# Differential attention and ternary FFN on one core: a head's difference, turns and copies half a head later, two-part fp16 scores

## The reference, cut to what matters

```python
q, k, v = LN(x) @ Wq.T, LN(x) @ Wk.T, LN(x) @ Wv.T      # 32 x 16, 16 x 16, 8 x 32
q, k = rope(q) * 16 ** -0.5, rope(k)
probs = softmax(q @ k.T + causal)                       # 32 score heads
diff = probs[:, :, 0] - lambda_full * probs[:, :, 1]    # 16 heads
attn = rmsnorm(diff @ v) * subln_weight * (1 - LAMBDA_INIT)
x = x + attn @ Wo.T
h = gelu(LN(x) @ ternary(w1).T + b1)
x = x + h @ ternary(w2).T + b2
```

## Time and profile before

| | |
|---|---|
| median of 3 runs | 4374.92 us |
| profiled execution, its own time | 4370.7 us |
| its span, first to last instruction | 4368.9 us |
| PE / DVE / ACT / POOL busy | 83 / 77 / 67 / 34 % |
| mean granted TensorE clock | 0.900 of 2.4 GHz |
| one image in the loop | 525.9 us |

### The profile page before, as it was taken

The page is one execution under the profiler, slowest core; times in us unless marked ns, Lnnn a source line. Parts: engine busy times, 40 slices in busy tenths (PEclk is TensorE's granted clock), DMA queues, the critical chain, the costliest instruction groups (busy, mean ns, idle before and its releaser), DMA issues.

```text
span 4368.9 us, 81035 instructions
## 1 busy us (share of the span) xinstructions
PE 3625.1 (83%) x23454; PEld 2157.1 (49%) x23454; DVE 3369.0 (77%) x6188; ACT 2913.5 (67%) x6786; POOL 1495.9 (34%) x1563
## 2 busy tenths in 40 slices
PE   2688888888888888888888988888888888888886
PEld 1345554455445454554545545555545555554553
DVE  6778967888678886788767887678877788678881
ACT  1567766777567775677756766667666777567772
POOL 0243234332333334332343324433134432333323
PEclk7788999989899899998889988999989989899998
DMA  4212112211122112212122110222122111222110
GB/s 133 54 25 41 24 43 43 40 23 33 35 43 43 23 38 46 43 25 38 26 43 43 36 31 23 47 37 43 25 44 43 32 31 25 44 43 43 20 37 14
DMA packets 146768, 166.71 MB, mean 38 GB/s; under 512 B 16640, under 2 KB 117632, under 8 KB 145792
## 3 DMA queue, kind: packets, MB, share of 16 engines
q1 hardware_dynamic: 146304, 161.13, 18.3%
HBM read 105.95 MB, written 55.12 MB: 37 GB/s over the span
## 4 chain that ended last, share of the span: by engine, by line
PE 41%; DVE 25%; issue 19%; ACT 8%; DMA 3%; SPq 2%; POOL 1%; DVEq 1%; ACTq 1%; POOLq 0%
DVE NM L667 9%; PE M L822 7%; PE M L872 7%; PE SP_ L837 6%; PE F L894 6%; PE DP L849 5%; PE F L907 4%; DVE E L691 3%; ACT E L543 3%; DVE CC L688 2%; DMA KST<-scratch 2%; PE M L816 2%; DVE NM L675 2%; PE SP_ L838 1%; PE DX L849 1%
## 5 line engine op out<-in xcount | busy, mean ns | idle before, releaser
L543 ACT ACTIVATE E<-SP_,NM 128x256 f32<-128x256 f32 (+7 forms) x2048 | 1518.3, 743 | 674.7 <-DVE NM L667 461.8
L667 DVE TENSOR_REDUCE NM<-SP_ 128x1 f32<-128x896 f32 (+3 forms) x1024 | 1034.2, 1018 | 257.8 <-PE SP_ L838 254.0
L837 PE MATMUL SP_<-KST,QST 96*128 96x512 bf16 (+3 forms) x3072 | 866.2, 356 | 394.5 <-ACT E L543 329.5
L691 DVE SCALAR_TENSOR_TENSOR E<-E,CC 128x512 f32<-128x512 f32 (+7 forms) x1024 | 928.6, 907 | 36.2
L555 ACT ACTIVATE DT<-DP 128x512 f32<-128x512 f32 (+3 forms) x1024 | 527.7, 515 | 534.9 <-PE DP L849 501.5
L849 PE MATMUL DP<-ident,E 128*128 128x128 f32 x3328 | 617.5, 304 | 140.4 <-DVE E L691 136.7
L675 DVE TENSOR_REDUCE NM<-SP_ 128x2 f32<-128x1024 f32 (+3 forms) x512 | 420.2, 821 | 309.2 <-PE SP_ L838 306.5
L837 PEld LDWEIGHTS SP_<-KST,QST 96*128 96x128 bf16 x3072 | 278.9, 103 | 745.7 <-ACT E L543 515.0
L894 PE MATMUL F<-X2H,W1Q 128*128 128x256 f16 x2048 | 512.1, 287 | 71.0 <-ACT HP L598 67.0
L849 PEld LDWEIGHTS DP<-ident,E 128*128 128x128 f32 x3328 | 395.6, 154 | 313.9 <-issue 164.3
L822 PE MATMUL M<-WQKV,WT 128*128 128x512 f32 x1040 | 531.7, 608 | 8.8 <-DVE T L650 4.1
(11 more groups left out here) (87 smaller groups left out, 4794.6 us busy)
## 6 DMA issues: line engine op xcount, KB each, us to landing
QST<-scratch SPq DMA_DIRECT2D x390, 128.0 KB, 4.4
scratch<-SPL SPq DMA_DIRECT2D x65, 576.0 KB, 2.8
KST<-scratch SPq DMA_DIRECT2D x390, 64.0 KB, 4.8
X<-in_x SPq DMA_DIRECT2D x66, 256.0 KB, 3.3
out<-SQ SPq DMA_DIRECT2D x64, 256.0 KB, 2.0
KST<-in_w1T SPq DMA_DIRECT2D x1, 4096.0 KB, 19.4
DT<-in_w2T SPq DMA_DIRECT2D x1, 4096.0 KB, 28.8
WQKV<-in_wqT SPq DMA_DIRECT2D x1, 1024.0 KB, 6.9
```

Source lines behind the costliest of these rows:

```text
L543: act.activation(dst, score_out(i, 2 * n + k, w), ACT.Exp, bias=NM[:, (2 * u + k) % 8:(2 * u + k) % 8 + 1], scale=1.0, accum_out=SUM[:, i ...
L667: nc.vector.tensor_reduce(NM[:, m:m + 1], score_out(i, 2 * n + k, P * (i + 1)), AX.X, ALU.max, negate=True).then_inc(max_ready, 1)
L691: nc.vector.scalar_tensor_tensor(out=E1[:, u % 2, 0:w], in0=E2[:, e:e + w], scalar=CC[:, u % 2:u % 2 + 1], in1=E1[:, u % 2, 0:w], op0=ALU. ...
L837: pe.matmul(SP_[:, k[a // 512], 0:n], q, KST[0:ROWS, a // P:(a + n) // P, kk, :], start=True, stop=not last)
```

## The change

Scores: q and k are split into two fp16 parts, high and rest, with scaled copies (rest times 64, high by 64), three products of 16 dimensions. Two score heads that share a KST column stand below each other (48 rows each), and QST holds zeros in the rows of the other one, so a score matmul still has 96 rows and the same columns. POOL's split becomes two `tensor_scalar`, the second from fp16 to fp16. The bytes of `QST`'s and `KST`'s DMAs halve at the same count of DMAs.

Order: `diff(s-1)` moves from h = 0 to h = 1 of step s; `diff_transposes(s-1)` from h = 1 of step s to h = 0 of step s+1; the copies go to h = 0 and h = 1 of that step; `half_v` follows half a step later. `E1` gets four rows, `E2` two in every tile, `R2` and `CC` four places. `exp(s,0)` waits for the turn of s-4 and `exp(s,1)` for `diff(s-2)`. The coefficient is still computed on DVE by the same two instructions.

Side jobs move one half step later, with these exceptions: `LN1_STATS`, `LN1_ROWS`, the FFN's places and `LN2_REST` (31) stay, `LN1_TURN` moves by two. Setup: w1 is loaded by four DMAs, as KST is half as large, and POOL clears QST. The diff, cut to its core:

```diff
-PROD = 6
-QPART = (0, 0, 0, 1, 1, 2)
-KPART = (0, 1, 2, 0, 1, 0)
-ROWS = PROD * DH
+PROD = 3
+QPART = (0, 2, 1)
+KPART = (0, 1, 2)
+PART = PROD * DH
+ROWS = 2 * PART
+LOW = 64.0
...
-LN1_STATS, LN1_ROWS, LN1_TURN = 1, 3, 4
-Q_PROJ, Q_ROPE = (7, 8, 9, 10), 11
-KV_PROJ, KV_ROPE = (12, 13, 14, 14), 15
-Q_TURN, Q_REST, K_TURN, K_REST = 16, 17, 20, 21
-V0_MOVE = 5
-PV_OUT = (19, 3)
-SUM_INVERSE, AT_TURN, AT_ROWS = 5, 6, 6
-MEAN_SQ, RMS_ROWS, AN_TURN = 9, 13, 22
-O_PROJ, O_SUM = (23, 24, 25, 26), 27
-LN2_STATS, LN2_ROWS, LN2_TURN, LN2_REST = 27, 29, 30, 31
+LN1_STATS, LN1_ROWS, LN1_TURN = 1, 3, 6
+Q_PROJ, Q_ROPE = (8, 9, 10, 11), 12
+KV_PROJ, KV_ROPE = (13, 14, 15, 15), 16
+Q_TURN, Q_REST, K_TURN, K_REST = 17, 18, 21, 22
+V0_MOVE = 6
+PV_OUT = (20, 4)
+SUM_INVERSE, AT_TURN, AT_ROWS = 5, 7, 7
+MEAN_SQ, RMS_ROWS, AN_TURN = 10, 14, 23
+O_PROJ, O_SUM = (24, 25, 26, 27), 28
+LN2_STATS, LN2_ROWS, LN2_TURN, LN2_REST = 28, 30, 31, 31
...
-        KST = sb("KST", [P, TILES, NK, P], BF16)
-        QST = sb("QST", [P, 2, NQ, P], BF16)
+        KST = sb("KST", [P, TILES, NK // 2, P], F16)
+        QST = sb("QST", [P, 2, NQ, P], F16)
         V = sb("V", [P, TILES, DKV], F32)
-        E1 = sb("E1", [P, 2, S], F32)
-        E2 = sb("E2", [P, S], F32)
+        E1 = sb("E1", [P, 4, S], F32)
+        E2 = sb("E2", [P, 2, S], F32)
         DT = sb("DT", [P, TILES, HALF, P], F32)
         NM = sb("NM", [P, 8], F32)
         SUM = sb("SUM", [P, 2, 2, H], F32)
-        R2 = sb("R2", [P, 2], F32)
+        R2 = sb("R2", [P, 4], F32)
         RS = sb("RS", [P, H], F32)
-        CC = sb("CC", [P, 2], F32)
+        CC = sb("CC", [P, 4], F32)
...
-        SPL = sb("SPL", [P, 3, D + DKV], BF16)
+        SPL = sb("SPL", [P, 3, D + DKV], F16)
...
-            sp.dma_start(w1f.rearrange("p (k n) -> p k n", k=KD), w1T.rearrange("(k p) n -> p k n", p=P)).then_inc(w1_in, 16)
-            sp.dma_start(w2f.rearrange("p (k n) -> p k n", k=FT), w2T.rearrange("(k p) n -> p k n", p=P)).then_inc(w2_in, 16)
+            for k in range(KD):
+                sp.dma_start(w1f[k], w1T[P * k:P * (k + 1), :]).then_inc(w1_in, 16)
+            sp.dma_start(draw.rearrange("p (k n) -> p k n", k=FT), w2T.rearrange("(k p) n -> p k n", p=P)).then_inc(w2_in, 16)
...
-                hold(sp, stacked, 16 * 2 * PROD * (nb - 1))
+                hold(sp, stacked, 64 * PROD * (nb - 1))
                 hold(sp, split_done, 2 * nb + 2)
                 sp.dma_start(scratch[tile % 2], SPL[:, :, :]).then_inc(scr_out, 16)
                 hold(sp, scr_out, 16 * nb + 16)
                 src = scratch[tile % 2].rearrange("(s d) a (c n) -> a d s c n", d=DH, n=P)
                 hold(sp, s_ready, q_free)
-                for j in range(PROD):
-                    sp.dma_start(QST[DH * j:DH * (j + 1), tile % 2, :, :].rearrange("p (s c) n -> p s c n", s=8),
-                                 src[QPART[j], :, :, 0:4, :]).then_inc(stacked, 16)
+                for a in range(2):
+                    for j in range(PROD):
+                        r = PART * a + DH * j
+                        sp.dma_start(QST[r:r + DH, tile % 2, :, :].rearrange("p (s c) n -> p s c n", s=8)[:, :, 2 * a:2 * a + 2, :],
+                                     src[QPART[j], :, :, 2 * a:2 * a + 2, :]).then_inc(stacked, 16)
                 if k_free is not None:
                     hold(sp, s_ready, k_free)
-                for j in range(PROD):
-                    sp.dma_start(KST[DH * j:DH * (j + 1), tile, :, :].rearrange("p (s c) n -> p s c n", s=8),
-                                 src[KPART[j], :, :, 4:6, :]).then_inc(stacked, 16)
+                for a in range(2):
+                    for j in range(PROD):
+                        r = PART * a + DH * j
+                        sp.dma_start(KST[r:r + DH, tile, :, :], src[KPART[j], :, :, 4 + a, :]).then_inc(stacked, 16)
...
+            pool.memset(QST[:, :, :, :], 0.0).then_inc(q_zeros, 1)
...
-                pool.tensor_scalar(SPL[:, 1, c], T2[:, c], 1.0, 0.0, ALU.mult, ALU.add).then_inc(mid_part, 1)
-                after(pool, mid_part, 2 * nb + part + 1)
-                pool.tensor_tensor(SPL[:, 2, c], T2[:, c], SPL[:, 1, c], ALU.subtract).then_inc(split_done, 1)
+                pool.tensor_scalar(SPL[:, 1, c], T2[:, c], LOW, 0.0, ALU.mult, ALU.add)
+                pool.tensor_scalar(SPL[:, 2, c], SPL[:, 0, c], 1.0 / LOW, 0.0, ALU.mult, ALU.add).then_inc(split_done, 1)
...
-                    old = T.before(n - 2)
+                    old = T.before(n - 4)
                     if old:
                         pb, pi, pn = old
                         after(act, t_ready, pb * N_T + tg(pi, pn, groups(pi) - 1) + 1)
-                    dst = E1[:, u % 2, 0:w]
+                    dst = E1[:, u % 4, 0:w]
                 else:
 
-                    after(act, d_ready, b * N_U + u - (1 if i < 4 and u > 0 else 0))
-                    e = 512 * (u % 2) if i < 4 else 0
-                    dst = E2[:, e:e + w]
+                    after(act, d_ready, b * N_U + u - 1)
+                    dst = E2[:, u % 2, 0:w]
...
-                    old = T.before(s - 1) if h else T.before(s - 2)
+                    old = T.before(s - 2)
                     if T.attend:
                         exp(T, s, h)
-                    if old and (h == 1 or groups(old[1]) == 2):
-                        dt_copy(*old, 1 - h)
+                    if old and (h == 0 or groups(old[1]) == 2):
+                        dt_copy(*old, h)
...
-                nc.vector.scalar_tensor_tensor(out=E1[:, u % 2, 0:w], in0=E2[:, e:e + w], scalar=CC[:, u % 2:u % 2 + 1],
-                                               in1=E1[:, u % 2, 0:w], op0=ALU.mult, op1=ALU.add).then_inc(d_ready, 1)
+                nc.vector.scalar_tensor_tensor(out=E1[:, u % 4, 0:w], in0=E2[:, u % 2, 0:w], scalar=CC[:, u % 4:u % 4 + 1],
+                                               in1=E1[:, u % 4, 0:w], op0=ALU.mult, op1=ALU.add).then_inc(d_ready, 1)
...
-                    if h == 0 and T.before(s - 1):
+                    if h == 1 and T.before(s - 1):
...
-                kk = ((s // 2) % 8) * 2 + (s // 2) // 8
+                kk = (s // 2) % 8
...
-                done = T.before(s - 2)
+                done = T.before(s)
...
-                    if h == 1:
-                        if T.before(s - 1):
-                            for g in range(groups(T.before(s - 1)[1])):
-                                diff_transposes(*T.before(s - 1), g)
-                        half_v(T, s, 1)
+                    if h == 0:
+                        if T.before(s - 2):
+                            for g in range(groups(T.before(s - 2)[1])):
+                                diff_transposes(*T.before(s - 2), g)
+                        half_v(T, s - 3, 1)
...
                     if h == 0:
                         scores_ahead(T, s + 1)
-                        half_v(T, s, 0)
+                    else:
+                        half_v(T, s - 2, 0)
```

More of the change, by code:

```diff
@@ L331, in diff_attention_ffn @@
         wsum = E1[:, 1, 0:2 * 64].rearrange("p (a b) -> p a b", b=64)
-        w1f = KST[:, :, :, :].rearrange("p a b c -> p (a b c)").bitcast(F32)
-        w2f = DT[:, :, :, :].rearrange("p a b c -> p (a b c)")
+        kraw = KST[:, :, :, :].rearrange("p a b c -> p (a b c)").bitcast(F32)
+        w1f = [kraw[:, 0:FF], kraw[:, FF:2 * FF], HH[:, :, :].rearrange("p a b -> p (a b)").bitcast(F32),
+               HL[:, :, :].rearrange("p a b -> p (a b)").bitcast(F32)]
+        draw = DT[:, :, :, :].rearrange("p a b c -> p (a b c)")
+        w2f = [draw[:, FF * k:FF * (k + 1)] for k in range(4)]
         cutt = HP[:, :, :].rearrange("p a b -> p (a b)")
@@ L412, in _ @@
             sp.wait_ge(w1_cut, 1)
+            sp.wait_ge(q_zeros, 1)
             stack(0, 0, 0, None)
@@ L778, in _ @@
             for j, (w, q, arrived) in enumerate(((w1f, W1Q, w1_in), (w2f, W2Q, w2_in))):
-                dve.wait_ge(arrived, 16)
-                link(nc.vector.tensor_reduce(wsum[:, j, :], w.rearrange("p (a c) -> p a c", a=64), AX.X, ALU.add,
-                                             apply_absolute_value=True))
+                dve.wait_ge(arrived, 64 - 48 * j)
+                for k in range(4):
+                    link(nc.vector.tensor_reduce(wsum[:, j, 16 * k:16 * k + 16], w[k].rearrange("p (a c) -> p a c", a=16), AX.X, ALU.add,
+                                                 apply_absolute_value=True))
                 nc.vector.tensor_reduce(wtot[:, j:j + 1], wsum[:, j, :], AX.X, ALU.add).then_inc(abs_sum, 1)
@@ L788, in _ @@
                     c = slice(FF * k, FF * (k + 1))
-                    link(nc.vector.tensor_scalar(cutt, w[:, c], thr[:, j, 1:2], None, ALU.is_le))
-                    ins = nc.vector.scalar_tensor_tensor(out=qf[:, c], in0=w[:, c], scalar=thr[:, j, 0:1], in1=cutt,
+                    link(nc.vector.tensor_scalar(cutt, w[k], thr[:, j, 1:2], None, ALU.is_le))
```

(1 more changed line is left out.)

15 lines of the change are left out of this document (7 added, 8 removed).

## The result

The kernel after takes 4360.7 us (median of eleven runs, 4358.32 to 4362.49), the kernel before, on the same chip, 4374.92 (eleven runs, 4368.63 to 4382.02). The ratio is 0.9966, with a 95% interval of 0.9957 to 0.9975: 14 us or 0.34% faster. The forecast was 4290. The sign came as predicted, the size did not: 84 us were expected. The profiled execution's span is 4359.0 us (before 4368.9) and the mean granted clock 0.913 of 2.4 GHz (before 0.900).

The account below looks back on a forecast made before the run. The bound was taken as a ring: PE's side jobs make scores late, DVE waits for them, then PE waits for the difference or exponential. Gains of 138 less costs of 54 gave 84 us off 4374.9, so 4290; range 4185 to 4400.

Parts of the forecast that it names:

- Side jobs move one half step later: Tile ends and starts: costs counted for X2H's wait, 28 us, and for the turns in successive half steps, 26 us.
- rival B: Whole run: the ring was the whole trouble, a third of DVE's score waits goes, 187 us, giving 4188; chance 0.22.
- rival D: Tile's tail and head become the wait at X2H and AT's turn, 173 us lost, giving 4433; chance 0.13.
- Term 5: Tile starts: stack lands 2 to 2.5 us sooner, POOL's split saves 0.4, chain starts 1.5 later; gain 22 us.
- Term 7: Tile ends: DVE waits 0.7 us for ACT's copy X2H at five of eight; cost 28 us.
- Term 8: Narrow tiles: TOK's turn, AT's turn and first projection in three successive steps cost 0.8 us each; cost 26 us.
- Terms 1 to 4 and 6: Gains: reciprocal's wait 30, PE's difference wait 23, copy AT 21, PE's half step per narrow tile 32, rope 10 us.
- term 2: PE's 136.7 us wait for a difference before turning it shrinks; gain 23 us.
- the granted clock: Some stretches run at 1.2 GHz instead of 2.4; which ones shift was unknown, 20 us allowed either way.
- C: Ring only turned: wide tiles unchanged, PE paces narrow ones; about 4365, between 4340 and 4384; chance 0.12.

Follow-up runs that it names:

- after_sum_27: Kernel after with the last two output projections packed at half step 26 and only LN2's sum and statistics moved forward to 27; 4304.42 us.
- s16_old_order: Kernel before with the change's new scores alone (two-part fp16, halved DMA bytes, POOL's shorter split), everything in the old order; 4318.81 us.
- after_x2h_first: Kernel after with ACT's copy X2H ahead of the tile's last exponential instead of behind it and its copy; 4336.26 us.
- after_all_three: Kernel after with TOK's turn at 5, the FFN's later first products, Gelus and splits one half step later, and after_tail_early's tail; 4263.05 us.
- after_two_banks: Kernel after with narrow tiles' transposes of a difference alternating between the banks DP and DX; 4361.13 us.
- after_tail_early: Kernel after with the last two output projections in one half step and LN2's sum, statistics, rows and turn one half step sooner; 4271.84 us.

## Why the prediction missed

The sum was 84 and the result is 14. By its steps:

- **The failed step: "Side jobs move one half step later", priced at X2H and the turns only.** The sentence of the change part that the FFN's places stay was read, and its consequence was not: O_SUM and LN2_STATS crossed the maximum of half step 28, which waits behind the second Gelu in wide odd tiles. The earlier trace rows showed a wait of the same kind (2.96 us, behind the first Gelu); it was cited as a lump that limits rival B, and what DVE did ahead of the second was not looked up. Moving the two back won 56 us (after_sum_27), of which tiles 5 to 7 are some 38 and tiles 1 to 3, where the root's wait went too, some 20. Nothing in the sum stood for it; rival D had the right place, the tile's tail, and another mechanism.
- **Term 5, the stack.** By the term's own numbers the new scores alone are worth 24 x (2 + 0.4) = 58 us, and 57 were measured (s16_old_order). From the first stack DMA's issue to KST's last landing it takes 10.8 us instead of 13.5 (medians from the traces), 2.6 less where 2 to 2.5 were let. The 36 us that the term takes off for a later start were never measured by themselves. Two slips: 2.5 + 0.4 - 1.5 is 1.4 and not 1.0, and the expectation for s16_old_order (4350 to 4365, a gain of 10 to 25) is as low as if the later start were still in it. POOL's second instruction did not become cheaper than the scale beside it but equal, 628 ns against 617, as the term's upper limit had it; about 5 us in all.
- **Term 7, X2H: 28 predicted, 24 measured** (after_x2h_first), and that is partly luck: the wait stands at all 64 tile ends and not at 40, is 0.5 us in wide tiles and 0.8 in narrow ones, and the run took away only 18 of the 43 us.
- **Term 8, the turns: 26 predicted, 8 measured** for the part that LN1_TURN 5 takes away. The rows (AT's 57 us, WT's 23) show the wait where it was put; no more than 8 us of time were found in it.
- **Terms 1 to 4 and 6, the order's gains: 116 predicted,** 80 with the later start of the stack taken off. The rows that were named moved as forecast, but they are not worth their sum. The order part as a whole costs 42; with 56 + 24 + 8 of costs measured one at a time, some 46 are left as gains, or up to 64 with term 8 at its full 26. after_all_three, 56 under s16_old_order, is in line with that. after_two_banks shows one reason: waits of PE ahead of the scores (term 2's among them, to 16.9 us) can go and win nothing. How the 46 to 64 divide among the five terms was not tried, and such sums hold only roughly, since the parts are not independent (the sum moved forward takes the root's wait with it).
- **The cost of POOL's root was not in the sum.** By the tiles it costs some 2 us per image, in narrow ones (above).

The ledger, then, which closes because the gains are its remainder: 84 - 1 (new scores, 58 against 57) - 56 (the omitted filler) + 4 + 18 (terms 7, 8) - 34 (gains less later start, 80 against 46) = 15, against 14 measured. That it closes proves nothing of the remainder.

One thing stands beside this ledger, the granted clock, for which the prediction let 20 us either way. It is 0.900 before, 0.911 in s16_old_order, 0.913 after, 0.918 in after_sum_27 and 0.919 in after_tail_early and after_all_three. Executions of the unchanged kernel before differ in the same sense: one at 0.906 took 4360.0 us, one at 0.896 took 4386.9, so 0.010 of clock goes with some 27 us. By that, up to half of the 57 us of the new scores may go with the clock, and some 13 of the 56 of after_sum_27. The order's loss of 42 does not, as the clock of the kernel after is no lower. Whether fewer waits raise the clock or the clock takes the waits away, no run here shows.

Of the rivals, C gave 4365 and lies nearest, but for a reason that is not the one: it took the late head for a turned ring without gain. With its side jobs in place the late head is faster (after_all_three), and the tail gave that back. B (4188) is refuted as far as it was reached: even after_all_three keeps 446.6 of DVE's 560.5 us.
